# Local attention of the layers: score products as 64x32 tiles of TensorE, 32 queries at a time, with shorter key ranges

## The reference

```python
def local_attention(q, k, v):              # w = WINDOW = 64, n = 256, nw = 4 windows
    bk2, bv2 = (look(bk), look(bv))        # window before and own window: 128 keys
    mask = (it < jb) | (it > jb + w) | (jb == -1)
    sim = jnp.einsum('bhwie,bhwje->bhwij', bq, bk2) * QK_SCALE
    sim = jnp.where(mask, -jnp.finfo(sim.dtype).max, sim)
    attn = jax.nn.softmax(sim, -1)
    return jnp.einsum('bhwij,bhwje->bhwie', attn, bv2)
```

## Time and profile before

| | |
|---|---|
| median of 3 runs | 3278.15 us (3271.11 to 3278.32) |
| profiled execution, span | 3280.4 us |
| PE busy | 3087.2 us (94%) |
| DVE, ACT, POOL busy | 2638.4, 2534.1, 2084.0 us |
| mean granted TensorE clock | 0.963 |
| front part | about 0 to 600 us |
| layers | about 600 to 3230 us |

### The profile page before, as it was taken

The page is one execution under the profiler, slowest core; times in us unless marked ns, Lnnn a source line. Parts: engine busy times, 40 slices in busy tenths (PEclk is TensorE's granted clock), DMA queues, the critical chain, the costliest instruction groups (busy, mean ns, idle before and its releaser), DMA issues. The chain is left out here.

```text
span 3280.4 us, 80720 instructions
## 1 busy us (share of the span) xinstructions
PE 3087.2 (94%) x29936; PEld 2736.1 (83%) x29936; DVE 2638.4 (80%) x5117; ACT 2534.1 (77%) x7059; POOL 2084.0 (64%) x1536
## 2 busy tenths in 40 slices
PE   5898886689999999999999999999999999999997
PEld 4666664479998999989999989999899998999996
DVE  3378888878789888788878898878988878888884
ACT  2787885478787888788888888888788887888784
POOL 5347655776666666666666676667676767666661
PEclk8888996799999999999999999999999999999998
DMA  3111100110001000001100011000100000110000
GB/s 128 55 36 49 59 4 7 42 36 11 2 2 34 25 26 2 2 21 33 31 2 2 11 34 39 1 2 2 37 26 22 2 1 21 33 31 7 8 5 26
DMA packets 27780, 75.04 MB, mean 23 GB/s; under 512 B 4120, under 2 KB 9848, under 8 KB 27256
## 3 DMA queue, kind: packets, MB, share of 16 engines
q1 hardware_dynamic: 22224, 52.63, 5.1%
q0 software_dynamic: 4864, 16.78, 1.6%
q10 hardware_dynamic: 304, 0.47, 0.1%
HBM read 65.68 MB, written 4.19 MB: 21 GB/s over the span
## 5 line engine op out<-in xcount | busy, mean ns | idle before, releaser
L1596 POOL TENSOR_TENSOR turned<-by_cos,turned 128x512 f32<-128x512 f32 x384 | 494.5, 1288 | 827.5 <-DVE turned L2101 827.0
L1600 POOL TENSOR_TENSOR rnorm<-norm,half 128x8 f32<-128x8 f32 x384 | 789.1, 2055 | 0.0
L1883 ACT ACTIVATE prob<-ps_s,ebias,rnorm 128x128 f32<-128x128 f32 x1536 | 681.8, 457 | 64.9 <-DVE ebias L2122 64.2
L2115 DVE TENSOR_REDUCE negmax<-ps_s 128x8 f32<-128x1024 f32 x192 | 235.0, 1224 | 284.0 <-PE ps_s L1698 283.9
L1892 ACT ACTIVATE prob_t<-ps_t 128x512 f32<-128x512 f32 x384 | 230.3, 600 | 223.4 <-PE ps_t L1707 218.8
L2130 DVE TENSOR_TENSOR prob<-prob,rinv 128x512 f32<-128x512 f32 x384 | 375.8, 979 | 13.1
L1642 PE MATMUL ps_qk<-w_hi,x_hi 128*128 128x512 f32 x768 | 336.8, 438 | 18.8 <-DVE turned L2101 12.2
L1787 PE MATMUL ps_f<-hid_hi,w_hi 128*128 128x256 f32 (+1 forms) x1056 | 309.3, 293 | 5.7 <-DVE hid_lo L2176 5.6
L1883 ACT ACTIVATION_READ_ACCUMULATOR prob<-ps_s,ebias,rnorm 128x1 f32 x1536 | 311.1, 203 | 0.0
L1642 PE MATMUL ps_qk<-w_lo,x_hi 128*128 128x512 f32 x768 | 305.8, 398 | 0.0
L1642 PE MATMUL ps_qk<-w_hi,x_lo 128*128 128x512 f32 x768 | 305.7, 398 | 0.0
(11 more groups left out here) (289 smaller groups left out, 9779.6 us busy)
## 6 DMA issues: line engine op xcount, KB each, us to landing
w_raw<-in_w_qkv SPq DMA_DIRECT2D x24, 768.0 KB, 4.8
w_raw<-in_w SPq DMA_DIRECT2D x12, 693.0 KB, 4.0
w_raw<-in_w_o SPq DMA_DIRECT2D x12, 512.0 KB, 3.4
w_raw<-in_w SPq DMA_DIRECT2D x6, 768.0 KB, 4.4
x_tok<-in_x SPq DMA_DIRECT2D x8, 256.0 KB, 2.7
kept<-x_t SPq DMA_DIRECT2D x8, 256.0 KB, 2.0
w_raw<-kept SPq DMA_DIRECT2D x8, 256.0 KB, 3.1
out<-rows_out SPq DMA_DIRECT2D x8, 256.0 KB, 2.2
```

The source lines that it names most:

```text
L1596: G.tensor_tensor(turned[:, k, :], by_cos[:, :], turned[:, k, :], ALU.add).then_inc(s["turned"], 1)
L1600: G.tensor_tensor(rnorm[:, i % RR, :], norm2[:, k, :], half[:, :], ALU.pow).then_inc(s["rnorm"], 1)
L1883: last = A.activation(prob[:, k, h, :], half_bank(h % 2, k)[:, T(h // 2)], ACT.Exp, bias=ebias[:, i // NU % 2, k, h:h + 1], scale=rnorm[:, ...
L2115: V.tensor_reduce(negmax[:, k, :, :].rearrange("p u (c o) -> p o u c", o=2), ps_s[:, :, :].rearrange("p o (u c k) -> p o u c k", u=NU, c=2 ...
```

## The change

The 64 queries of a half are split into two of `QW` = 32 (`part` 0 and 1 are the lower, 2 and 3 the upper queries). The tile of the array is 64x32 (`tile_position=(DH * odd, QW * part)`), so there are eight tile places instead of four. Parts 2 and 3 take only the 96 keys that their queries can see (0 to 95 and 32 to 127 of the unit); in the first unit part 0 takes 32 keys and part 1 takes 64. In the second unit parts 0 and 1 keep 128 keys. What is left out is masked anyway. A group has 32 products (64 records and 64 weight loads) in place of 16 (32 and 32). The mask matmuls (L1679) stay at 64x64 tiles.

```diff
+QW = WIN // 2
             for u in range(NU):
                 for c in range(GH // 2):
-                    for upper in range(2):
+                    for part in range(4):
                         for odd in range(2):
                             rows = slice(DH * odd, DH * odd + DH)
-                            first = u * P + upper * WIN
-                            q_win = qk_t[rows, c, first:first + WIN]
+                            q_part = qk_t[rows, c, u * P + part * QW:][:, 0:QW]
                             k_all = qk_t[rows, 2 + c, :]
-                            o = half_bank(odd, u)[upper * WIN:(upper + 1) * WIN, T(c)]
-                            if upper:
-                                k_win = k_all[:, T(u)]
+                            o = half_bank(odd, u)[part * QW:(part + 1) * QW, T(c)]
+                            if part >= 2:
+                                seen = slice((part - 2) * QW, (part + 1) * QW)
+                                k_seen, o = k_all[:, T(u)][:, seen], o[:, seen]
                             elif u:
-                                k_win = k_all[:, WIN:WIN + P].rearrange("p (w k) -> p w k", w=2)[:, ::-1, :]
+                                k_seen = k_all[:, WIN:WIN + P].rearrange("p (w k) -> p w k", w=2)[:, ::-1, :]
                                 o = o.rearrange("p (w k) -> p w k", w=2)
                             else:
-                                k_win, o = k_all[:, 0:WIN], o[:, 0:WIN]
-                            last = E.matmul(o, q_win, k_win, start=False, stop=True, skip_group_check=True)
+                                seen = slice(0, (part + 1) * QW)
+                                k_seen, o = k_all[:, seen], o[:, seen]
+                            last = E.matmul(o, q_part, k_seen, start=False, stop=True, skip_group_check=True,
+                                            tile_position=(DH * odd, QW * part))
```

## The result

The changed kernel takes 3286.77 us (median of 13 runs, 3277.68 to 3294.28) against 3273.16 us of the kernel before in the same series: ratio 1.0035, interval 1.0023 to 1.0047, that is 11.5 us slower (7.5 to 15.4; the medians differ by 13.6). I had forecast 3268.5, ten us faster.

What follows compares the result with a forecast made beforehand. PE was taken to bound the kernel. The terms took the score block from 1215 to 1165 ns, 50 ns saved in each of 192 groups, 9.6 us off 3278.15, giving 3268.5 us; range 3257 to 3286.

Steps and rivals of the forecast that it cites:

- What bounds the kernel: Whole kernel: PE sets the time, so a nanosecond saved in the score block counts once for each of 192 groups.
- Item 1: Score products: with fewer columns streamed in eight places, the longest chain falls from 872 to about 664 ns, -208 ns.
- Items 2, 3 and 4: Between mask and products: new change of tile size +90 ns, exposed first load +24 ns, later start of last tile +47 ns.
- Rival A: Score products: tiles start closer, 3.3 ns apart, as entries queue during the mask; 74 ns saved, 3264 us; chance 0.13.
- Item 5: PE's sequencer: 64 more loads and matmuls cost nothing, since 128 entries at 1.7 ns take 213 ns, less than 664.
- Rival C: Later in the step: the gain is swallowed by waits PE meets there, leaving 0 to 6 us, 3272 to 3278; chance 0.13.
- Rival D: Products' slots: eight streams exceed what array or memory ports feed at full rate; slower, 3295 or 3386 us; chance 0.18.

Runs made afterwards that it cites:

- pause-only kernel: The kernel before with only its mask in eight 64x32 tiles, which adds a change of tile size before the 64x64 products; block 1.374 us.
- narrow: The changed kernel with 64 keys at most for every 32 queries, other key products left out; block 1.110 us, layers 2567.9 us.
- pause taken out: The changed kernel with the mask in 64x32 tiles as well; block 1.108 us, layers 2578.6 us, ratio 0.9961 of the kernel before.
- mask and reversed order: The changed kernel with mask in 64x32 tiles and products ordered second unit first, parts 3, 2, 1, 0; block 1.088 us, ratio 0.9947.
- either order alone: The changed kernel, only products reordered: four places first, block 1.292 us, ratio 1.0051; or second unit first, parts 3 to 0, block 1.247 us.

## Why the prediction was wrong, point by point

- **What bounds the kernel:** right. Where the block changed by a lot, the layers followed: +160 ns gave +25.7 us in the pause-only kernel (30.7 by the product with 192), -104 gave -22 (narrow), -106 gave -11 (pause taken out; see there for the clock), -126 gave -20 (mask and reversed order).
- **Item 1, columns:** the slots were right (83 ns, 109 ns, eight side by side at full rate), and so was the streaming time of the longest chain, 664 ns, which is eight such slots.
- **Items 2, 3 and 4,** pause, load, start of the last tile: right to 10 ns, by the records after and by the kernel with the pause alone. Rival A is out (6.7 ns, not 3.3).
- **Item 5 failed.** I let the sequencer hand over an entry every 1.7 ns, which is how closely the first records start after a pause, 213 ns for 128 entries, and booked nothing. That rate is that of entries already in the reserve. Products from behind it come at 16 to 17 ns each at best, 23.5 on the mean, and not at the 4 x 1.7 = 6.7 I had booked. Comparing the sum of all entries with the streams was wrong as well: even at 4.2 ns an entry 128 entries are 538 ns, less than 664. What counts is when the last products come, and those come late because an entry waits until the one 64 before it, and all before that, have ended. The stretch became 714 instead of 652 ns (+62), its end another 7: 1234 instead of 1165. Sixteen products as before never showed it: they are 64 entries, no more than the reserve, and 872 ns of streams for 16 products need only one every 54 ns.
- **The end:** 50 ns saved became 20 lost, and 28 more outside the block: +48 ns x 192 = 9.2 us, the 10.8 of the layers with the groups at either end. The 28 are in part shown (the wait before L1741) and in part open (`hidden_mm`, the wait before L1667). Rival C put the swallowing into waits before L1667, L1741 and L1800; the first two are where it came, but it added to a loss.
- **Rival D** had the sign, and by the stretch even the size ((714 - 71) / 7 = 92 ns a slot, above its break-even of 89), with the wrong mechanism: the slots stayed at 83 and 109 ns, and what ran short was the supply of products. Its argument against, that four streams ran at full rate, was sound and beside the point. On the chances: I gave a slower time 0.18, though item 5 rested on no row of a long run of short products.

The Trainium skill, "TensorE: Matmul & The Clock Gate", in its table at the head, gives TensorE a queue of 64 instructions with partial reorder. In the change and in the kernels with narrower products and with either order alone, the first 64 entries (16 products with two loads and two matmuls each) start without waiting for their supply, and the first late load is behind them: the trace agrees. I had not weighed it.

## What to carry to other kernels

When tiles are made smaller, count not only columns and pauses but products: twice the places with half the work each need twice the entries in the same time, and here the queue hid that for 64 entries only. Beyond them an entry waits for the end of the one 64 before it, so what stands in front of a long run of small products should end early. Give neighbours on TensorE the same tile size; here the mask in the products' tiles turned +0.35% into -0.39%, and a better order into -0.53%. And when a small change is timed, look at the stretch that holds it: the span of one execution moved by more in the untouched front part than the whole effect.

## What the runs showed of the hardware that I had not expected

- After the first 17, fp32 products of 64x32 tiles reach TensorE at 16 to 17 ns each at best, 4.2 ns an entry; why at that rate no run shows. The same 64x32 tiles stream at full rate in eight places when products are long enough (109 ns slots, a stretch of 0.847 us).
- The refill waits for the front of the queue: the first load of the 18th product comes at 277, 327 or 381 ns, in each case 31 to 32 ns after the modelled end of the 1st product (245, 296, 349).
- Across a change of tile size no weight load runs ahead: with the mask in 64x64 tiles and the products in 64x32 the first load starts 338 ns after the first mask matmul, with both in 64x64 tiles after 27 ns.
- Within the queue the places run ahead of each other: the fourth record of part 0 starts at 116 ns, before the second of parts 2 and 3 at 134 to 154, which come earlier in the program.
